# A decoder layer with a mixture of experts: cross attention with unpacked token rows joined in, and the order of the first expert loads

## The chip, the cores and the metric

The kernel runs on one core of one Trainium2 chip. The metric is the device time in microseconds (us) of one execution. Engines are named as in the profile: PE is TensorE, ACT is ScalarE, DVE is VectorE, POOL is GpSimd, SP is SyncE, which here only issues DMAs.

## The reference, cut to what matters

Two sequences of 1024 tokens with 256 features go through self-attention, cross attention (16 heads, 64 keys) and a mixture of 16 experts, each followed by a residual sum and a layer norm. What the change touches is the router and what follows it:

```
x = layernorm(x + xattn(x, ctx, mask))               # x2 of the kernel
logits = x @ router_w + router_b                      # 16 experts
probs  = softmax(logits)
topw, topi = top_k(probs, 4)
topw = topw / sum(topw)
out[token] = sum over its 4 experts e of topw_e * (gelu(x @ w1[e] + b1[e]) @ w2[e] + b2[e])
x = layernorm(x + out)
```

## The kernel before

The 2048 tokens are 16 tiles of 128 (NT = 16). The kernel has these stages: setup and projections, self-attention, cross attention with the router, a table of expert steps, the expert loop, and a last norm. Every engine has its own program; they meet through counting semaphores.

**Cross attention** is a software pipeline. On each engine the function `pipeline(engine, 16, [(skew, fn), ...])` runs steps t = 0, 1, ...; in step t it calls `fn(t - skew)` in the listed order, if that tile exists. The list is thus the order of the work on that engine, and the largest skew says how many steps follow the last tile. The first steps are written out, the middle ones run in a hardware loop in which tile numbers are registers, and the last ones are written out again. An optional `ramp` list holds for the first `RAMP` steps.

For tile t, on PE: `cquery` (skew 0), `cscores` (1, line 799 begins it), `cturn_p` (2), `cattend` (2, line 821), `turn_o` and `project` (3), then with x2 known `turn_x2` (4), `logits` (4), and `positions` (6), which counts with two small matmuls how many earlier tokens chose each expert. On DVE: `head_max`, `sub_max` (1), `head_inv`, `head_norm` (2), the second norm (3, `residual2` to `norm2`, whose inverse root is `root2` on POOL), and the router (4 to 6): logits, their maximum, the probabilities, the four largest, a one-hot mask, the shares, the rows, and `indices`. ACT copies PSUM results to SBUF and takes exponentials (`cexps`, `rexps`).

**Dispatch.** Each token row has to be written to four places of the DRAM buffer `expert_rows`, one for each of its experts. ACT's `pack` copies the tile four times into the buffer `xd` (two tiles deep), where DVE puts beside each copy the token's own number (column D) and its share for that expert (column D + 1). POOL's `dispatch` (skew 6) issues four indirect DMAs for each tile, 16 x 4 in all (line 563). `pack` of tile t and `indices` of tile t wait until the four scatters of tile t - 2 have landed, because they reuse its buffers.

**Between the stages.** DVE makes a table `tab` (18 small steps) of which rows and which expert each expert step takes. PE sums each token's shares times b2 (`turn_shares`, `bias_sums`, in two halves), ACT copies the sums to `total`, SP stores the first half (2 x 512 KB, after `xb` 4) and ACT the second (2 x 512 KB). SP then loads w1 and w2 of the first expert, waits for all scatters, and loads the rows of the first two expert steps (`load_rows`).

**Expert loop**, up to 48 steps, 40 here, each with 256 rows of one expert (w1, w2, rows loaded two steps ahead by SP): `turn_g`, `up`, gelu, `down`. ACT's `y_out` scales each result row by its share, `home_on[:, p, c, 1:2]`, and POOL adds the rows to `expert_sum` by an indirect DMA (line 582). POOL's first of these waits until all stores of the sums have landed. `y_out` also waits for the scatters of two steps before.

```
def done(t):      return t + 1 + BIAS       # semaphore value when tile t is done
def freed(t):     return t + 1              # when tile t - 2 is done
def upto(t, n):   ...                       # t + n, at most the last tile
```

## Time and profile before

| | us |
|---|---|
| median of 3 runs (lowest, highest) | 618.08 (615.75, 623.73) |
| the profiled execution, its own time | 615.27 |
| its span in the profile | 613.5 |
| PE busy in the span | 526.4 (86%) |
| DVE, ACT, POOL busy | 422.0, 344.0, 286.2 |

The span is the time from the first to the last instruction of the profiled execution. The page also gives a chain of work that ended last (PE 68%, DMA 7%, DVE 7%, POOL 4%, ACT 3%), and its strip of 40 slices shows PE's busy share at nine tenths nearly throughout, with a dip in slices 20 and 21, about 291 to 322 us, in which PE's clock is at its lower level too. A matmul's end is modelled, so PE can look busy where it is not at its peak.

### The profile page before, as it was taken

The page shows a single profiled execution, that of the slowest core. Times are in us where ns is not written, and L with a number is a line of the kernel's source. Part 1 is how long each engine was busy: PE and PEld are TensorE (multiplying, and loading weights), DVE is VectorE, ACT ScalarE, POOL GpSimd, SP SyncE. Part 2 cuts the span into 40 slices and gives each one's busy share as a digit, 9 for nine tenths or more (in the row PEclk, how much of TensorE's full clock was granted, in tenths as well). Part 3 has the DMA queues.
Part 4 walks back from the last instruction along what each step waited for, and adds up shares of the span by engine and source line. Part 5 has one row for each costly group of instructions (what it writes and reads, how often), then busy time and mean ns, then how long its engine had stood idle before and what let it go on. Part 6 is the DMA issues. An engine that isn't in the chain of part 4 may idle for free.

```text
span 613.5 us, 14428 instructions
## 1 busy us (share of the span) xinstructions
PE 526.4 (86%) x4048; PEld 497.8 (81%) x4048; DVE 422.0 (69%) x1053; ACT 344.0 (56%) x633; POOL 286.2 (47%) x264
## 2 busy tenths in 40 slices
PE   5999999999779999996327999999999999999700
PEld 4988888888669988886226999999999999999600
DVE  2646655555467888886534988888888787888336
ACT  2433333333235666664234777788778877778504
POOL 6551111111120356666640355666676767676733
PEclk9999999999989999999556999999999999999955
DMA  8799999400000132322387799999999999998477
GB/s 274 269 399 398 396 396 398 154 0 0 1 1 2 37 109 73 114 96 105 118 279 244 204 251 264 259 253 260 257 258 258 258 258 254 256 257 220 48 200 236
DMA packets 91836, 124.42 MB, mean 203 GB/s; under 512 B 6737, under 2 KB 62993, under 8 KB 91809
## 3 DMA queue, kind: packets, MB, share of 16 engines
q1 hardware_dynamic: 75264, 103.40, 51.4%
q0 software_dynamic: 14592, 19.41, 15.8%
q10 hardware_dynamic: 1952, 1.28, 0.8%
q8 instruction: 13, 0.21, 0.1%
q14 instruction: 15, 0.11, 0.1%
HBM read 61.93 MB, written 62.14 MB: 202 GB/s over the span
## 4 chain that ended last, share of the span: by engine, by line
PE 68%; issue 8%; DMA 7%; DVE 7%; POOL 4%; ACT 3%; POOLq 0%; SPq 0%; DVEq 0%; ACTq 0%
PE ps L347 18%; PE ps L349 18%; PE ps L348 18%; DMA expert_rows<-xd,idx 4%; POOL expert_rows L563 3%; PE ps L931 3%; PE ps L748 2%; PE ps L821 1%; DMA expert_sum<-yb,home_row 1%; PE ps L811 1%; PE ps L782 1%; DMA x_all<-in_x 1%; PE ps L852 1%; DMA total<-expert_sum 1%; PE ps L803 1%
## 5 line engine op out<-in xcount | busy, mean ns | idle before, releaser
L582 POOL DMA_INDIRECT expert_sum<-yb,home_row x80 | 163.1, 2039 | 107.4 <-DVE home_row L1513 62.3
L347 PE MATMUL ps<-gT_h,w_h 128*128 128x256 f32 x320 | 94.8, 296 | 1.8 <-issue 1.3
L347 PE MATMUL ps<-w_h,h_h 128*128 128x256 f32 x320 | 90.8, 284 | 1.9 <-DVE h_l L1506 1.9
L348 PE MATMUL ps<-gT_l,w_h 128*128 128x256 f32 x320 | 91.6, 286 | 0.0
L349 PE MATMUL ps<-gT_h,w_l 128*128 128x256 f32 x320 | 91.5, 286 | 0.0
L349 PE MATMUL ps<-w_h,h_l 128*128 128x256 f32 x320 | 90.6, 283 | 0.0
L348 PE MATMUL ps<-w_l,h_h 128*128 128x256 f32 x320 | 90.6, 283 | 0.0
L563 POOL DMA_INDIRECT expert_rows<-xd,idx x64 | 62.6, 978 | 33.4 <-issue 22.3
L1506 DVE TENSOR_TENSOR h_l<-hf,h_h 128x1024 fp32r<-128x1024 f32 x40 | 49.0, 1226 | 38.0 <-ACT h_h L1138 37.7
L1131 ACT ACTIVATE hf<-ps,b1s 128x256 f32<-128x256 f32 x160 | 62.8, 480 | 19.7 <-PE ps L349 19.3
L347 PEld LDWEIGHTS ps<-gT_h,w_h 128*128 128x128 f32 x320 | 62.2, 194 | 2.4 <-issue 1.5
L347 PEld LDWEIGHTS ps<-w_h,h_h 128*128 128x128 f32 x320 | 61.4, 192 | 2.4 <-DVE h_l L1506 2.4
L348 PEld LDWEIGHTS ps<-gT_l,w_h 128*128 128x128 f32 x320 | 62.3, 195 | 0.0
L349 PEld LDWEIGHTS ps<-gT_h,w_l 128*128 128x128 f32 x320 | 62.2, 194 | 0.0
L349 PEld LDWEIGHTS ps<-w_h,h_l 128*128 128x128 f32 x320 | 61.5, 192 | 0.0
L348 PEld LDWEIGHTS ps<-w_l,h_h 128*128 128x128 f32 x320 | 61.5, 192 | 0.0
L536 POOL TENSOR_TENSOR rstd<-ve,mhalf 128x1 f32<-128x1 f32 x16 | 8.8, 550 | 104.4 <-DVE ve L1209 104.4
L1113 ACT ACTIVATE yb<-ps,home_on 128x256 f32<-128x256 f32 x80 | 33.5, 470 | 37.9 <-DMA expert_sum<-yb,home_row 30.9
L1480 DVE TENSOR_TENSOR w_l<-w1f,w_h 128x1024 fp32r<-128x1024 f32 x40 | 49.0, 1225 | 1.4
L1485 DVE TENSOR_TENSOR w_l<-w2f,w_h 128x1024 fp32r<-128x1024 f32 x40 | 48.7, 1216 | 0.7 <-ACT w_h L1124 0.7
L347 PE MATMUL ps<-v_h,pT_h 128*128 (+1 forms) x128 | 37.1, 290 | 7.3 <-ACT x1T L1026 5.6
L1138 ACT ACTIVATE h_h<-hf 128x1024 fp32r<-128x1024 f32 x40 | 42.4, 1060 | 1.3
(241 smaller groups left out, 1342.7 us busy)
## 6 DMA issues: line engine op xcount, KB each, us to landing
expert_rows<-zeros SPq DMA_DIRECT2D x32, 1088.0 KB, 13.8
w1f<-in_L_ffn_w SPq DMA_DIRECT2D x40, 512.0 KB, 4.8
w2f<-in_L_ffn_w SPq DMA_DIRECT2D x40, 512.0 KB, 6.1
xg<-expert_rows SPq DMA_DIRECT2D x40, 272.0 KB, 3.9
total<-expert_sum SPq DMA_DIRECT2D x16, 256.0 KB, 5.8
x_all<-in_x SPq DMA_DIRECT2D x8, 256.0 KB, 6.9
expert_sum<-x_all SPq DMA_DIRECT2D x8, 256.0 KB
out<-ot SPq DMA_DIRECT2D x8, 256.0 KB, 2.6
```

The source lines that it names most:

```text
L347: pe.matmul(o, ah, bh, start=first, stop=False)
L348: pe.matmul(o, ah, bl, start=False, stop=False)
L349: return pe.matmul(o, al, bh, start=False, stop=last)
L563: pool.indirect_dma_start(out=xg_dram, out_offset=bass.IndirectOffsetOnAxis(ap=idx[:, p, r:r + 1], axis=0), in_=xd[:, p, r], in_offset=Non ...
L582: pool.indirect_dma_start(out=sums[p], out_offset=bass.IndirectOffsetOnAxis(ap=home_row[:, p, c:c + 1], axis=0), in_=yb[:, p, c], in_offse ...
L931: mm = pe.transpose(ps[:, p, kc * SLOT + c * P:kc * SLOT + (c + 1) * P], xg[:, p, c, kc * P:(kc + 1) * P], ident[:])
L1113: ins = act.activation(yb[:, p, c], ps[:, 6 + p, c * D:(c + 1) * D], ACT.Copy, scale=home_on[:, p, c, 1:2])
L1131: ins = act.activation(hf[:, p, j], ps[:, 2 + 2 * p + j // 2, (j % 2) * SLOT:(j % 2 + 1) * SLOT], ACT.Gelu, bias=b1s[:, j, ds(t, 1)])
L1138: act.activation(h_h[:, p], hf[:, p], ACT.Copy).then_inc(hh, 1)
L1480: dve.tensor_tensor(w1_l[:, p], w1f[:, p], f(w1_h[:, p]), ALU.subtract).then_inc(w1l, 1)
L1485: dve.tensor_tensor(w2_l[:, p], w2f[:, p], f(w2_h[:, p]), ALU.subtract).then_inc(w2l, 1)
L1506: dve.tensor_tensor(h_l[:, p], hf[:, p], f(h_h[:, p]), ALU.subtract).then_inc(hl, 1)
```

## The change

One row of `x_all`, 288 values wide, now holds a tile's token with all that its scatters need: 256 features, its 16 shares (columns D to D + E - 1, zero where an expert wasn't chosen) and its number (column HOME = D + E). `xd` and `pack` are gone: all four scatters of a tile send the same row of `x_all`, and `idx` has a place for every tile, so nothing waits for earlier scatters. `y_out` picks its share from 16 columns with the expert's number, which ACT loads into a register. The router works on logits: the largest four are found on them, ACT negates the first (`neg_max`), and a second exponential (`top_sum`) sums the four. `positions` moves from skew 6 to 4 (another PSUM bank), `dispatch` and `indices` from 6 to 5, `head_inv` and `head_norm` from 2 to 3 at the head of DVE's step, `turn_x2` from 4 to 3 at the end of PE's step. POOL's steps are all written out, and in the last ones half a tile's scatters go before `root2`. `bias_sums` of the first half comes after the last tile's `positions` instead of the third last's. ACT's order changes, with `q_out` ahead of `cexps` in a ramp of 4 steps. SP loads w2 of the first expert after the first two sets of rows, and stores the second half of the b2 sums itself, after w1 of the second step.

```diff
-RW = D + 16
+RW = D + 2 * E
+HOME = D + E
...
-RAMP = 3
+RAMP = 4
...
-        x_all = sb("x_all", [P, NT, D])
+        x_all = sb("x_all", [P, NT, RW])
+        idx = sb("idx", [P, NT, K], U32)
...
-        home_i = sbe("home_i", [P, 2, K], I32)
+        home_i = sbe("home_i", [P, NT], I32)
...
-        idx = sbe("idx", [P, 2, K], U32)
-        xd = sbe("xd", [P, 2, K, RW])
...
@@ SyncE @@
             first = expert_of(0)
             load_up(0, 0, first)
-            load_down(0, 0, first)
...
             for t in range(2):
                 load_rows(t, t, places[t])
+            load_down(0, 0, first)
...
                     load_up(t, p, expert_of(t))
+                if isinstance(t, int) and t == 1:
+                    sp.wait_ge(xb, 8)
+                    for b in range(B):
+                        store_tiles(sp, sums[1], total, b * TPB + 4, 4)
...
@@ GpSimd @@
-            pool.memset(xd[:], 0.0).then_inc(c_pool, 1)
+            pool.memset(x_all[:, :, D:RW], 0.0).then_inc(c_pool, 1)
...
-            pool.tensor_copy(xd[:, :, :, D], home_i[:]).then_inc(c_pool, 1)
+            pool.tensor_copy(x_all[:, :, HOME], home_i[:]).then_inc(c_pool, 1)
...
+            def send(t, p, k, r):
+                pool.indirect_dma_start(
+                    out=xg_dram, out_offset=bass.IndirectOffsetOnAxis(ap=idx[:, t, r:r + 1], axis=0),
+                    in_=x_all[:, p * TPB + k], in_offset=None).then_inc(sc_dma[p][r], 16)
+
+            def ready(t):
+                pool.wait_ge(lidx, done(t))
+                pool.wait_ge(lsh, done(t))
+                pool.wait_ge(x2k, done(t))
+                pool.sem_inc(passed, 1)
...
+            def dispatch_first(t, p, k):
+                ready(t)
+                for r in range(K // 2):
+                    send(t, p, k, r)
+
+            def dispatch_rest(t, p, k):
+                for r in range(K // 2, K):
+                    send(t, p, k, r)
+
+            steady = [(1, causal), (3, root2), (5, dispatch)]
+            ending = [(5, dispatch_first), (3, root2), (5, dispatch_rest)]
...
-            pipeline(pool, NT, [(1, causal), (3, root2), (6, dispatch)])
+            for t in range(NT + 5):
+                for skew, fn in steady if t < NT + 1 else ending:
+                    if 0 <= t - skew < NT:
+                        fn(t - skew, (t - skew) % 2, (t - skew) // 2)
...
@@ TensorE @@
             def turn_o(t, p, k):
                 pe.wait_ge(co, done(t))
                 pe.wait_ge(coc, freed(t) + 1)
+                if not (isinstance(t, int) and t < 2):
+                    pe.wait_ge(lcar, done(t - 2))
...
             def project(t, p, k):
...
-                if not (isinstance(t, int) and t < 4):
-                    pe.wait_ge(lcar, done(t - 4))
+                pe.wait_ge(x2t, freed(t) + 1)
...
-                    mm = pe.transpose(ps[:, 4, D + kc * P:D + (kc + 1) * P], xs[:, p, kc * P:(kc + 1) * P], ident[:])
+                    mm = pe.transpose(ps[:, 7, D + kc * P:D + (kc + 1) * P], xs[:, p, kc * P:(kc + 1) * P], ident[:])
...
-                if isinstance(t, int) and t == NT - 3:
+                pe.wait_ge(coc, done(upto(t, 1)))
+                pe.matmul(ps[:, 6, D:D + E], tri_r[:], mk[:, p], start=True, stop=True)
+                pe.matmul(ps[:, 6, D + E:D + 2 * E], ones_r[:], mk[:, p], start=True, stop=True).then_inc(pos_ps, 1)
+                if isinstance(t, int) and t == NT - 1:
                     pe.wait_ge(cpc, done(NT - 1))
                     bias_sums(0, 0)
...
-            pipeline(pe, NT, [(1, cscores), (3, turn_o), (4, turn_x2), (2, cturn_p), (6, positions), (3, project),
-                              (0, cquery), (4, logits), (2, cattend)])
+            pipeline(pe, NT, [(1, cscores), (4, logits), (3, turn_o), (2, cturn_p), (3, project), (0, cquery),
+                              (2, cattend), (4, positions), (3, turn_x2)])
...
@@ ScalarE @@
-            def pack(t, p, k):
-                act.wait_ge(x2k, done(t))
-                if not (isinstance(t, int) and t < 2):
-                    for r in range(K):
-                        act.wait_ge(sc_dma[p][r], 16 * k)
-                act.sem_inc(passed, 1)
-                act.activation(xd[:, p, :, 0:D], x_all[:, ds(p * TPB + k, 1), :].broadcast_to([P, K, D]), ACT.Copy).then_inc(xdc, 1)
...
+            def neg_max(t, p, k):
+                act.wait_ge(l8, done(t))
+                act.activation(lmax[:, p:p + 1], mx8[:, p, 0:1], ACT.Copy, scale=-1.0).then_inc(lmx, 1)
...
-                act.activation(lexp[:, p], lg[:, p], ACT.Exp, bias=lmax[:, p:p + 1], accum_out=lsum[:, p:p + 1]).then_inc(lex, 1)
+                act.activation(lexp[:, p], lg[:, p], ACT.Exp, bias=lmax[:, p:p + 1]).then_inc(lex, 1)
...
+            def top_sum(t, p, k):
+                act.wait_ge(lwi, freed(t))
+                act.activation(top[:, p], mx8[:, p, 0:K], ACT.Exp, bias=lmax[:, p:p + 1], accum_out=wsum[:, p:p + 1]).then_inc(lws, 1)
...
-            pipeline(act, NT, [(3, o_out), (4, x2_turned), (2, p_out), (1, cexps), (0, q_out), (5, pack), (4, keep_x2), (4, rexps)],
-                     ramp=[(3, o_out), (4, x2_turned), (2, p_out), (0, q_out), (1, cexps), (5, pack), (4, keep_x2), (4, rexps)], ramp_steps=RAMP)
+            pipeline(act, NT, [(4, x2_turned), (4, keep_x2), (3, o_out), (2, p_out), (4, neg_max), (4, rexps), (1, cexps), (4, top_sum), (0, q_out)],
+                     ramp=[(4, x2_turned), (4, keep_x2), (3, o_out), (2, p_out), (0, q_out), (4, neg_max), (4, rexps), (1, cexps), (4, top_sum)], ramp_steps=RAMP)
...
-            act.wait_ge(xb, 8)
-            for b in range(B):
-                store_tiles(act, sums[1], total, b * TPB + 4, 4)
...
             def y_out(t, p, k):
...
+                expert = act.value_load(tab[1:2, ds(t, 1)], min_val=0, max_val=E - 1)
...
-                    ins = act.activation(yb[:, p, c], ps[:, 6 + p, c * D:(c + 1) * D], ACT.Copy, scale=home_on[:, p, c, 1:2])
+                    ins = act.activation(yb[:, p, c], ps[:, 6 + p, c * D:(c + 1) * D], ACT.Copy, scale=home_on[:, p, c, ds(expert, 1)])
...
@@ VectorE @@
-            def logits_max(t, p, k):
-            def router_inv(t, p, k):
-            def router_probs(t, p, k):
...
-                dve.max(mx8[:, p], rp[:, p]).then_inc(l8, 1)
+                dve.max(mx8[:, p], lg[:, p]).then_inc(l8, 1)
...
-                dve.tensor_reduce(wsum[:, p:p + 1], mx8[:, p, 0:K], AX.X, ALU.add).then_inc(lws, 1)
...
+            def share_sum(t, p, k):
+                dve.wait_ge(lws, done(t))
+                dve.reciprocal(winv[:, p:p + 1], wsum[:, p:p + 1]).then_inc(lwi, 1)
+
             def all_shares(t, p, k):
-                dve.wait_ge(lmk, done(t))
-                dve.scalar_tensor_tensor(shares[:, ds(p * TPB + k, 1), 0:E].rearrange("p a e -> p (a e)"), rp[:, p], winv[:, p:p + 1],
+                dve.wait_ge(lwi, done(t))
+                dve.wait_ge(lex, done(t))
+                dve.scalar_tensor_tensor(shares[:, ds(p * TPB + k, 1), 0:E].rearrange("p a e -> p (a e)"), lexp[:, p], winv[:, p:p + 1],
+                                         f(mk[:, p]), ALU.mult, ALU.mult).then_inc(lst, 1)
+                dve.scalar_tensor_tensor(x_all[:, ds(p * TPB + k, 1), D:D + E].rearrange("p a e -> p (a e)"), lexp[:, p], winv[:, p:p + 1],
                                          f(mk[:, p]), ALU.mult, ALU.mult).then_inc(lsh, 1)
...
-                for r in range(K):
-                    if not (isinstance(t, int) and t < 2):
-                        dve.wait_ge(sc_dma[p][r], 16 * k)
-                dve.tensor_copy(idx[:, p], slotf[:, p]).then_inc(lidx, 1)
-                dve.tensor_scalar(xd[:, p, :, D], xd[:, p, :, D], float(P), None, ALU.add).then_inc(dest, 1)
-                dve.wait_ge(lwi, done(t))
-                dve.tensor_scalar(xd[:, p, :, D + 1], mx8[:, p, 0:K], winv[:, p:p + 1], None, ALU.mult).then_inc(lw, 1)
+                dve.tensor_copy(idx[:, ds(t, 1), :].rearrange("p a r -> p (a r)"), slotf[:, p]).then_inc(lidx, 1)
...
-            pipeline(dve, NT, [(5, router_inv), (1, head_max), (5, router_probs), (1, sub_max), (5, largest), (3, residual2),
-                               (5, chosen), (3, stats2), (5, chosen_float), (6, rows_of), (3, aggr2), (6, next_rows), (5, one_hot),
-                               (3, var2), (6, pick_rows), (5, chosen_mask), (6, slots), (5, all_shares), (6, indices),
-                               (3, norm2), (2, head_inv), (2, head_norm), (4, logits_out), (4, logits_max)])
+            pipeline(dve, NT, [(3, head_inv), (5, rows_of), (3, head_norm), (5, next_rows), (5, pick_rows), (5, slots), (5, indices),
+                               (1, head_max), (4, logits_out), (4, largest), (1, sub_max), (3, residual2), (4, chosen), (3, stats2),
+                               (4, chosen_float), (3, aggr2), (4, one_hot), (3, var2), (4, chosen_mask), (4, share_sum), (4, all_shares),
+                               (3, norm2)])
...
-                dve.tensor_copy(home[:, p], xg[:, p, :, D:D + 2]).then_inc(hm, 1)
+                dve.tensor_copy(home[:, p], xg[:, p, :, D:HOME + 1]).then_inc(hm, 1)
```

## Rows read from the trace of the kernel before

**Rows 1.** Busy time by stretch: us, PE, PEld, DVE, ACT, POOL busy, clock, DMA share, GB/s

```profile
310.00:320.00 10.00, 2.22 (x10) 1.87 (x10) 1.10 (x6) 2.08 (x5) 4.36 (x5) 0.50 1.00 315
...
360.00:560.00 200.00, 200.00 (x1682) 200.00 (x1682) 167.06 (x259) 157.08 (x291) 134.72 (x64) 1.00 0.99 257
```

**Rows 2.** Timeline of PE in cross attention: start, length, instruction, idle before

```profile
181.22 0.50 PE L799 MATMUL ps<-hide_r,ones_r 64*128 64x512 f32 x2
...
182.51 0.44 PE L828 MATMUL ps<-ident,octx 128*128 128x128 f32 x2
...
205.54 1.95 PE L821 MATMUL ps<-vb,cpT 128*128 128x34 f32 x16
...
219.32 1.95 PE L821 MATMUL ps<-vb,cpT 128*128 128x34 f32 x16
...
269.78 1.95 PE L821 MATMUL ps<-vb,cpT 128*128 128x34 f32 x16
271.67 0.51 PE L799 MATMUL ps<-hide_r,ones_r 64*128 64x512 f32 x2
```

**Rows 3.** Waits from 205 to 280 us: who for whom, total, times, longest

```profile
ACT xd L1076 <- DMA expert_rows<-xd,idx: 16.4, 10, 2.0
```

**Rows 4.** Timeline of ACT, cross attention, before its loop

```profile
183.86 1.02 ACT L1049 ACTIVATE cpT<-ps 128x1024 f32<-128x1024 f32 x1 [0.49 <-PE ps L811]
...
195.02 0.31 ACT L1084 ACTIVATE lexp<-lg,lmax 128x16 f32<-128x16 f32 x1 [2.24 <-DVE lmax L1350]
195.24 0.19 ACT L1084 ACTIVATION_READ_ACCUMULATOR lexp<-lg,lmax 128x1 f32 x1
...
204.70 1.06 ACT L1059 ACTIVATE prob<-prob 128x1024 f32<-128x1024 f32 x1 [0.28 <-DVE prob L1304]
```

**Rows 5.** Timeline of DVE, before its loop

```profile
182.63 1.23 DVE L1299 TENSOR_REDUCE hmax<-ps 128x16 f32<-128x1024 f32 x1 [0.59 <-PE ps L803]
...
186.27 0.15 DVE L1335 TENSOR_SCALAR ve<-mv 128x1 f32<-128x1 f32 x1
...
206.54 0.23 DVE L1391 SCALAR_TENSOR_TENSOR shares<-rp,winv,mk 128x16 f32<-128x16 f32 x1
206.69 0.16 DVE L1418 CAST idx<-slotf 128x4 uint32<-128x4 f32 x1
```

**Rows 6.** Timeline of DVE, inside its loop

```profile
235.53 0.23 DVE L1391 SCALAR_TENSOR_TENSOR shares<-rp,winv,mk 128x16 f32 x1
235.83 0.17 DVE L1418 CAST idx<-slotf 128x4 uint32<-128x4 f32 x1
```

**Rows 7.** Timeline of POOL, the last tiles

```profile
286.31 1.04 POOL L563 DMA_INDIRECT expert_rows<-xd,idx  x1 [0.82 <-issue]
287.65 0.96 POOL L563 DMA_INDIRECT expert_rows<-xd,idx  x1 [0.30 <-issue]
...
292.29 0.57 POOL L553 TENSOR_TENSOR rstd<-ve,mhalf 128x1 f32<-128x1 f32 x1 [1.14 <-DVE ve L1335]
```

**Rows 8.** Chain of waits into the expert loop: start, length, what

```profile
290.18 2.46 DMA expert_rows<-xd,idx
...
314.62 7.18 DMA expert_rows<-xd,idx
322.16 2.94 DMA xg<-expert_rows
```

**Rows 9.** Issues of SP's queue: start, length, DMA

```profile
309.45 0.98 SPq L354 DMA_DIRECT2D expert_sum<-total  x2
313.24 0.40 SPq L415 DMA_DIRECT2D w1f<-in_L_ffn_w  x1
```

**Rows 10.** Timeline of DVE, the end of the step table

```profile
311.38 0.20 DVE L1467 CAST tab<-ps 2x48 int32<-2x48 f32 x1 [0.47 <-PE ps L915]
```

**Rows 11.** Issues of SP in the expert loop

```profile
363.37 0.38 SPq L410 DMA_DIRECT2D xg<-expert_rows  x1
364.65 0.37 SPq L415 DMA_DIRECT2D w1f<-in_L_ffn_w  x1
```

More of the change, by code:

```diff
@@ L279, in decoder_layer @@
         xg = sbl("xg", [P, 2, 2, RW])
-        home = sbl("home", [P, 2, 2, 2])
-        home_on = sbl("home_on", [P, 2, 2, 2])
+        home = sbl("home", [P, 2, 2, E + 1])
+        home_on = sbl("home_on", [P, 2, 2, E + 1])
         home_row = sbl("home_row", [P, 2, 2], U32)
@@ L817, in cattend @@
                 pe.wait_ge(co, freed(t) + 1)
-                if not (isinstance(t, int) and t < 3):
-                    pe.wait_ge(lgb, done(t - 3))
+                if not (isinstance(t, int) and t < 2):
+                    pe.wait_ge(lgb, done(t - 2))
                 for g, pair in enumerate(SCORED):
@@ L826, in turn_o @@
                 pe.wait_ge(coc, freed(t) + 1)
+                if not (isinstance(t, int) and t < 2):
+                    pe.wait_ge(lcar, done(t - 2))
                 for kc in range(KD):
@@ L848, in project @@
                 pe.wait_ge(cres, freed(t) + 1)
-                if not (isinstance(t, int) and t < 4):
-                    pe.wait_ge(lcar, done(t - 4))
+                pe.wait_ge(x2t, freed(t) + 1)
                 for kc in range(KD):
```

70 lines of the change are left out of this document (25 added, 45 removed).

## The prediction

> **What bounds the kernel now.** I read the busy time by stretch first. In the expert loop, 360 to 560 us, PE is busy all 200 us, ACT only 157.08 [rows 1]; the stretch holds 1682 matmuls at 52 a step (48 and 4 transposes), so 32.3 steps of 6.19 us, and PE sets them. Nothing of the change is PE work there. From 310 to 320 us PE works 2.22 of 10 us while the DMA engines are busy all the time [rows 1]: the expert loop can't start before the last scatters have landed and the first rows are loaded. That gap is what the change can shorten.
>
> The timeline of PE shows cross attention. Its steps, from one `cattend` (line 821) to the next, last 6.89 us before the loop of registers ((219.32 - 205.54) / 2) and 7.21 us in it ((269.78 - 219.32) / 7) [rows 2]. The waits name the reason: ACT's `pack` stood 16.4 us, in 10 waits, for scatters of two tiles before [rows 3].
>
> The last tiles on POOL show the real chain: a scatter takes 0.96 us with 0.30 to the next, the first after a `root2` comes 0.82 after it [rows 7]. A tile costs 1.34 + 2 x 1.26 + 0.96 = 4.8 us, and `pack` and `indices` wait for landings on top, until the last scatter starts at 314.62. It lands 7.18 us later, one at 290.18 took 2.46; then SP issues `xg` at 322.16, which lands after 2.94, and PE starts at 325.1 [rows 8].
>
> **Cross attention's steps.** Removed on ACT: `pack`, and its wait. Removed on DVE: six small instructions (maximum, inverse, probabilities, sum, two on `xd`); added: a second `all_shares`. ACT gains `neg_max` and `top_sum`. The new order makes a cycle that I add from the start of `cscores` (line 799). PE comes to `turn_o` 1.29 later [rows 2], now with `logits` between (0.35, my estimate for two transposes' worth of work): 1.64. From `turn_o` to ACT's `p_out` takes 183.86 - 182.51 = 1.35 [rows 2, 4]: 2.99. `p_out` 1.0, `neg_max` and `rexps` 0.22 each by the small exponential's step from 195.02 to 195.24 [rows 4]: 4.4. `cexps` 1.0, `top_sum` 0.22 and its accumulator read 0.19 [rows 4]: 5.8. This read is what `share_sum` waits for on DVE. Its reciprocal 0.2, two `all_shares` at 0.15 each [rows 5], the norm 0.4, `turn_x2` 0.2 on PE, and `cscores` follows: 6.95. PE's own work is the 6.89 of above. In the loop an instruction with a register in its address costs DVE 0.30 instead of 0.15 to the next [rows 5, 6]; two such and the norm behind them add 0.3, so 7.25. Seven or eight loop steps go from 7.21 to 7.25, and some written-out steps get 0.06 and one `positions` (0.2) more: **0.5 us lost** by the last step. Bounds: 6.89 everywhere would gain 7 x 0.32 = 2.2; 7.6, if the waits between engines add up, would lose about 4.
>
> POOL isn't the limit there: `root2` 0.57, gap 0.82, scatters 4.8, together 6.2 us [rows 7]. Its addresses are plain numbers, all steps being written out.
>
> **The last tiles.** Step 16 starts at 271.67 [rows 2]. `ve` comes 1.41 + 3.64 us after `cscores` began (182.63 - 181.22, 186.27 - 182.63) [rows 2, 5], with the router's parts between 0.1 more, so `root2` of tile 13 starts at 276.9. Tile 11's scatters: 278.3 to 283.1. Two of tile 12: 283.4 to 285.7. `root2` of tile 14 to 286.2; before, it ended 0.82 ahead of 286.31, at 285.5 [rows 7]. Two of tile 12 from 287.1, two of tile 13 from 289.6 to 291.9. `root2` of tile 15 started at 292.29 before [rows 7]; now its tile is held 0.7 by the former `root2` and 0.4 by `logits`, put ahead: 293.4. Rest of 13: 294.8 to 297.1. Tile 14: 297.4 to 302.2. Tile 15: 302.5, its last scatter starts at 306.4. The rows of 14 and 15 are ready by about 295 and 300, so POOL sets this. That is 8.2 us ahead of 314.62: one tile less was left, and two landings are no longer waited for.
>
> **The landing.** Before, two stores of 512 KB by SP were issued at 309.45, two by ACT after them, w1 at 313.24 and w2 behind it [rows 9]: 3 MB around the last scatter, which took 4.7 us more than the one at 290.18 [rows 8]. After, the first half of the sums follows the last tile's `positions`. I put it at 304.3, the table at 305.2, w1 at 306.9 (as 311.58 to 313.24 before [rows 9, 10]). So 1.5 MB lie around the scatter. Bounds are 2.46 and 7.18; the nearer row is the crowded one, since the stores precede the scatters by as little. I take 5.2, so 311.6. The rows' load comes 0.36 later and takes 2.94 [rows 8]: PE starts at 314.9, **10.2 us earlier**. Against this stands a rule. The Trainium skill, "DMA: Bandwidth & Descriptors", section "Queues, rings and completion order", says that each DMA engine goes round between the queue rows that have work, a packet at a time. By it what slows a scatter is that another queue is active, not how many bytes it holds; the rival below prices this from rows.
>
> w1 lands in time: issued at 306.9, even with 7.18 it is there at 314.1 and DVE's split is over before `up`, which needs the turned rows, some 2.5 us behind 314.9. PE's granted clock was 0.50, the 1.2 GHz level, from 310 to 320 [rows 1], after a stretch with little PE work; I leave it so in the first `up`.
>
> **w2 and the late stores.** SP now issues w2 at about 312.9, w1 of step two, then 1 MB of sums. 1.5 MB move to where the loop's first loads are. At the 315 GB/s of rows 1 they take 4.8 us. w2 is needed only by the first gelu's stage, 8 us after the rows, and the sums only by POOL's first accumulation, over 20 us later. The third rows, behind the stores, may be late: 0 to 2 us, I take **0.5 lost**. If that cover is gone, `gelus`, queued behind `w2_high` on ACT, waits, and `down` with it.
>
> **The expert loop.** `y_out` gets a `value_load` on ACT. The trace of ACT has none; SP's load of rows to load of w1 holds one, 364.65 - 363.37 - 0.38 = 0.90 us with two waits [rows 11]. I take 0.9 as the dearest likely, below it 0. ACT has (200 - 157.08) / 32.3 = 1.33 idle a step [rows 1], part of it a wait for a landing that comes behind the load, so the 40 steps lose nothing; the last result pays it: **0.9 lost**. The Trainium skill, the same page, section "Latency and other measured facts", gives a floor of about 0.6 us for a tensor load; by it the last step would pay 0.6, an estimate from that page. Rows of 288 instead of 272 values add 16 KB a step, 1% of what the DMA engines move in 6.19 us at 257 GB/s [rows 1], with loads two steps ahead: nothing; with no such cover 0.06 a step, 2.5. `home` with 34 instead of 4 columns stays under 0.1 on DVE, which is idle 33 of 200 us. The zeros' 6% more ends long before cross attention. Setup saves POOL one long memset, which nobody waits for.
>
> **Sum.** 10.2 - 0.5 - 0.5 - 0.9 = 8.3 us. Against the profiled execution's 615.27 (span 613.5) this is 607.0. The median of the runs stands 2.8 above that execution; from 618.08 it is 609.8. I say **608**, chance 0.38, own range 605.5 to 611.
>
> **Rivals.**
> - All covers hold: the step is 6.89 (+2.7 against my loss of 0.5), the landing 2.7 (+2.5), no crowding (+0.5), the load hidden (+0.4). 14.4 us, **602**. For it speaks that the wait of rows 3 goes. 0.22.
> - The landing stays at 7.18, since any active queue slows the scatter (the rule above): 2 us less, **610**. 0.18.
> - The cross step is set by the way over `top_sum`: at 7.6 us, 11 steps lose 0.4 each instead of 0.5 in all: **612**. Against it: ACT has over 2 us free in such a step once `pack` is gone. 0.10.
> - The reordering doesn't do what it says: w2 and the sums only move the crowd behind the rows, the first gelu waits for w2. A landing of 7.18 from 312.9, then `w2_high` and the gelu's table, ends just at `up`'s end; 3 us more cost 3: **611**. 0.07.
> - Slower: the `value_load` on ACT holds the loop. It decides from 1.33 us on; at 1.54 the 8.3 are gone (8.3 / 40 = 0.21), at 1.85 the kernel is over 2% slower, at 2.0 it takes 27 - 8 = 19 more, **636**. Against it: the 0.90 of rows 11. 0.05.
>
> **The numbers.** Range: 601 takes in most of the first rival, 614 the second to fourth; outside are the slow rival and the ends. 2% of 618.08 is 12.4 us, about what a measurement can tell from no change, so faster means below 605.7: nearly all of the first rival and the forecast's edge, 0.27. Slower 0.04. Same 0.69.
>
> **What would show it.** `cattend` to `cattend` in the loop (7.25); last scatter's start (306.4) and landing (5.2); PE's first transpose of rows (314.9); the expert step (6.19); ACT's gap before the last `yb`. I am wrong if POOL waits between the last tiles' scatters, if the step is off by over 0.2, or if the expert step grows.

## The result, and the profile after

| | before | after |
|---|---|---|
| median of 20 runs each, same chip (us) | 616.74 | 613.66 |
| lowest, highest | 614.85, 623.73 | 608.77, 623.99 |
| the profiled execution (span) | 615.27 (613.5) | 613.05 (611.2) |
| PE, DVE, ACT, POOL busy | 526.4, 422.0, 344.0, 286.2 | 535.9, 419.1, 336.2, 289.8 |

The ratio is 0.9935, 95% interval 0.9911 to 0.9959: 4.0 us faster, between 2.5 and 5.5 (3.1 by the medians), where 8.3 were forecast. The time of the new kernel lies in the range of 601 to 614, at its upper end, 5.7 us above the 608 that I said. Times of one kernel fall into groups some 3 us apart, each with its own mean granted clock (after: 612.03 to 614.57 at 0.931 to 0.937, 616.67 to 617.31 at 0.926 to 0.928), so below a span is read with its clock and steps are compared one by one, and each ratio is of the executions within 1.5% of their kernel's fastest.

The page of after: busy time of each engine, then slices of 15.3 us with PE's busy tenths and its granted clock.

```profile
PE 535.9 (88%) x4048; PEld 501.5 (82%) x4048; DVE 419.1 (69%) x973; ACT 336.2 (55%) x650; POOL 289.8 (47%) x264
...
PE   5999999999779999999648999999999999999600
...
PEclk9999999999989999978657999999999999999955
```

PE is busy 9.5 us longer with the same 4048 matmuls. No matmul was added; some ran at the lower clock. The slice with a 7 in the clock's strip, 260 to 275 us, is in the middle of cross attention, where the page of before has a 9.

**Cross attention.** PE's timeline, `cattend` (now line 839), the counterpart of [rows 2]:

```profile
235.68 1.87 PE L839 MATMUL ps<-vb,cpT 128*128 128x34 f32 x16
...
242.93 1.87 PE L839 MATMUL ps<-vb,cpT 128*128 128x34 f32 x16
...
257.63 1.87 PE L839 MATMUL ps<-vb,cpT 128*128 128x34 f32 x16
...
268.36 1.87 PE L839 MATMUL ps<-vb,cpT 128*128 128x34 f32 x16
...
275.42 1.87 PE L839 MATMUL ps<-vb,cpT 128*128 128x34 f32 x16
...
278.01 0.50 PE L817 MATMUL ps<-hide_r,ones_r 64*128 64x512 f32 x2
```

Steps of 7.25 and (257.63 - 242.93) / 2 = 7.35, then one of 10.73, then 7.06; the last row is `cscores` of step 16 (line 817), 271.67 before. The windows of that stretch (us, PE, PEld, DVE, ACT, POOL busy, clock, DMA share, GB/s) say what the long one is:

```profile
258.00:260.00 2.00, 1.84 (x17) 1.75 (x17) 1.74 (x12) 1.02 (x4) 1.11 (x2) 1.00 0.01 2
...
262.00:264.00 2.00, 2.00 (x10) 1.35 (x9) 1.22 (x2) 0.00 (x0) 1.63 (x2) 0.50 0.38 148
...
266.00:268.00 2.00, 2.00 (x9) 1.64 (x9) 0.21 (x1) 1.97 (x4) 0.00 (x0) 0.62 0.00 0
```

The clock is 1.00 (2.4 GHz) to 260 us, 0.50 (1.2 GHz) about 261 to 267, and 1.00 again. One step's matmuls take twice as long, and the step is 10.73 - 7.45 = 3.28 us longer than its neighbour. PE had been busy 1.84 of the 2 us before the fall.

The chain of waits gives the terms of an ordinary step in the loop (start, length, what):

```profile
231.03 0.50 PE ps L817 x2
...
232.95 0.26 PE ps L848 x2
...
234.12 0.04 ACT cpT L1067
...
235.49 0.04 ACT prob L1077
...
236.44 0.38 ACT top L1105 x2
...
236.84 0.17 DVE winv L1394
...
237.46 0.42 DVE xs L1358
...
237.92 0.44 PE ps L882 x2
```

It is the cycle of the forecast: scores, logits, `turn_o`, ACT's `p_out`, two small ACT instructions, `cexps`, `top_sum`, DVE's reciprocal, shares and norm, and PE's transposes of x2. PE's own order closes it: `turn_x2` ends its step, and the next `cscores` stands behind it.

In the written-out steps, 7.12 to 7.15 us long, the chain is put down to PE alone, but there too `turn_x2` starts only when DVE's norm is done, at 194.20:

```profile
193.79 0.41 DVE L1358 TENSOR_SCALAR xs<-yres,mv,rstd 128x256 f32<-128x256 f32 x1
```

```profile
194.26 0.44 PE L882 MATMUL ps<-ident,xs 128*128 128x128 f32 x2
```

The chain's piece for the logits, and PE's weight loads for them (idle before in brackets):

```profile
195.99 0.55 PE ps L890 x4
196.54 0.27 PE ps L848 x2
```

```profile
195.92 0.52 PEld L890 LDWEIGHTS ps<-rw,x2T 128*128 128x128 f32 x4 [0.33 <-issue]
```

The weights of the logits are loaded only after a gap of 0.33, which PE then sees: 0.55, where the same piece takes 0.35 in experiment 7.

**The last tiles.** POOL's timeline: the first scatter of tile 11, `root2` of tile 15, the last scatter. It answers to [rows 7].

```profile
284.48 1.14 POOL L558 DMA_INDIRECT expert_rows<-x_all,idx  x1 [0.27 <-DVE x_all L1401]
...
299.72 0.57 POOL L555 TENSOR_TENSOR rstd<-ve,mhalf 128x1 f32<-128x1 f32 x1 [1.56 <-DVE ve L1352]
...
312.06 0.96 POOL L558 DMA_INDIRECT expert_rows<-x_all,idx  x1 [0.30 <-issue]
```

From tile 11's first scatter to the last are 27.6 us (312.06 - 284.48), against 28.1 forecast (306.4 - 278.3). All of it merely starts late. The clock falls once more here, to 0.57 from 284 to 292 us, where before kept 1.00 until 288; PE's last step lies in it, 8.50 us long (6.94 before).

**Into the loop.** The chain of waits, the counterpart of [rows 8], then SP's issues, that of [rows 9], and PE's transposes of expert rows:

```profile
312.06 4.81 DMA expert_rows<-x_all,idx
...
323.15 6.43 DMA xg<-expert_rows
```

```profile
310.39 0.94 SPq L352 DMA_DIRECT2D expert_sum<-total  x2
...
317.23 1.00 SPq L408 DMA_DIRECT2D xg<-expert_rows  x2
...
320.65 1.01 SPq L352 DMA_DIRECT2D expert_sum<-total  x2
323.15 0.69 SPq L408 DMA_DIRECT2D xg<-expert_rows  x1
```

```profile
320.11 2.21 PE L949 MATMUL ps<-ident,xg 128*128 128x128 f32 x8 [6.67 <-DMA xg<-expert_rows]
...
329.63 1.12 PE L949 MATMUL ps<-ident,xg 128*128 128x128 f32 x4 [2.58 <-DMA xg<-expert_rows]
...
337.10 0.60 PE L949 MATMUL ps<-ident,xg 128*128 128x128 f32 x4
...
343.29 0.60 PE L949 MATMUL ps<-ident,xg 128*128 128x128 f32 x4
```

The last scatter lands in 4.81 us, not 7.18. PE has rows at 320.11, 5.0 us earlier than before. The third rows are issued behind the sums at 323.15 and take 6.43 us: PE waits 2.58. The expert step is 6.19 (343.29 - 337.10), as before. The steady loop starts from 337.10, which in the trace of before reads

```profile
340.10 0.60 PE L931 MATMUL ps<-ident,xg 128*128 128x128 f32 x4
```

so 3.0 us are left there, and 2.3 at the end. ACT's last results but one, after and before (idle ahead in brackets):

```profile
574.53 0.84 ACT L1130 ACTIVATE yb<-ps,home_on 128x256 f32<-128x256 f32 x2 [0.93 <-PE ps L347]
```

```profile
576.70 0.84 ACT L1113 ACTIVATE yb<-ps,home_on 128x256 f32<-128x256 f32 x2 [0.22 <-PE ps L349]
```

The `value_load` shows as the 0.93 against 0.22: 0.7 us.

### The profile page after: what moved, and what is told of

The parts are those of the page before. It is cut to its first block, busy times and chain, and to the rows that moved or that the text cites. A ratio compares the mean times of both kernels' runs of the same rounds, so it can differ in the third digit from the quotient of the medians.

```text
span 611.2 us, 14540 instructions
## 1 busy us (share of the span) xinstructions
PE 535.9 (88%) x4048; PEld 501.5 (82%) x4048; DVE 419.1 (69%) x973; ACT 336.2 (55%) x650; POOL 289.8 (47%) x264
## 4 chain that ended last, share of the span: by engine, by line
PE 75%; issue 7%; DVE 5%; DMA 4%; POOL 4%; ACT 3%; SPq 1%; ACTq 0%; POOLq 0%; DVEq 0%
PE ps L345 19%; PE ps L347 18%; PE ps L346 18%; PE ps L949 3%; POOL expert_rows L558 3%; PE ps L821 2%; PE ps L829 2%; PE ps L768 2%; PE ps L839 1%; PE ps L890 1%; PE ps L817 1%; DMA xg<-expert_rows 1%; PE ps L800 1%; PE ps L882 1%; DMA x_all<-in_x 1%
## 5 line engine op out<-in xcount | busy, mean ns | idle before, releaser
L602 POOL DMA_INDIRECT expert_sum<-yb,home_row x80 | 167.4, 2093 | 103.5 <-DVE home_row L1514 81.7
L558 POOL DMA_INDIRECT expert_rows<-x_all,idx x64 | 63.3, 989 | 19.0 <-issue 17.2
L1141 ACT ACTIVATE w_h<-w2f 128x1024 fp32r<-128x1024 f32 x40 | 42.7, 1067 | 1.7 <-DMA w2f<-in_L_ffn_w 1.7
```

The lines of the kernel that those rows point to most:

```text
L558: pool.indirect_dma_start(out=xg_dram, out_offset=bass.IndirectOffsetOnAxis(ap=idx[:, t, r:r + 1], axis=0), in_=x_all[:, p * TPB + k], in_ ...
L602: pool.indirect_dma_start(out=sums[p], out_offset=bass.IndirectOffsetOnAxis(ap=home_row[:, p, c:c + 1], axis=0), in_=yb[:, p, c], in_offse ...
L1141: act.activation(w2_h[:, p], w2f[:, p], ACT.Copy).then_inc(w2h, 1)
```

## The experiments

Each is compared with the kernel before on the same chip. Where a short name helps, "the change" is the changed kernel.

**1. The norm ahead of the shares.** One edit of the change's list on DVE:

```diff
-  (4, chosen_mask), (4, share_sum), (4, all_shares), (3, norm2)])
+  (4, chosen_mask), (3, norm2), (4, share_sum), (4, all_shares)])
```

> The changed kernel with one move on DVE: norm2 comes before share_sum and all_shares. Theory A (the cycle through top_sum and the two shares sets the step): the norm no longer waits for ACT's accumulator read; what is left is root2 (ve at 236.42, root2 to 237.23, norm2 at 237.26 at the earliest where it began at 237.46), so the step goes from 7.35 to 7.15 us in the loop, the last scatter starts 2 us earlier, and the time falls by about 2 us, or by about 5 if the low-clock step at 260 to 269 us goes too. Rival B (POOL's root2, not the shares, holds the norm): the step stays at 7.3 and the time within 0.5 us of the changed kernel.

Measured: 615.56 us median of 12, ratio 0.9934 (0.989 to 0.9978), the change's own. In the profile (of the execution of 618.34) steps written out went from 7.13 to 7.04, in the loop from 7.45 and 7.25 to 7.30 to 7.43 and 7.06 to 7.24. The terms behind `top_sum` were worth 0.1 to 0.2 us only: with them out of its way, the norm starts little earlier, since it now waits for POOL's `root2` (0.45 to 0.47 us, idle DVE). That is the rival's reason, though not its 7.3. The cycle over PE has to be cut elsewhere.

**2. PE's waits filled.** Three transposes of the identity into a free place, ahead of `turn_x2`'s wait for x2:

```diff
+  pe.wait_ge(cqc, done(upto(t, 3)))
+  for i in range(3):
+      pe.transpose(ps[:, 4, D:D + P], ident[:], ident[:])
```

> The changed kernel with three extra 128-column transposes on PE, into unused PSUM, ahead of turn_x2's wait: 0.33 us of work where PE otherwise waits for the norm, for each of 16 tiles. Theory C (PE's waits in the longer step are what lets its granted clock fall to 1.2 GHz for one step, 3.3 us, in most executions): the low-clock step in cross attention goes in the profile, most runs lie near the single fastest run of the changed kernel (608.8), and the time falls by 2 to 3 us though PE does 5 us more work. Rival D (the drop has another cause): it stays, and the time is the same or up to 2 us longer.

Measured: 612.07 median of 7, ratio 0.9884 (0.9813 to 0.9954); four at 609.45 to 612.07 with clock 0.941 to 0.948, three at 618.82 to 620.52 with 0.924 to 0.926. In the profile, which is of the 618.82, the loop's steps are 7.26 and 7.45 to the last, none long. A step of 10.19 is the very first, at the entry to cross attention; the very last is long too (8.25, its `cattend` 3.47 for 1.87). A window at the place where the change's clock falls:

```profile
262.00:266.00 4.00, 3.89 (x35) 3.60 (x36) 3.54 (x21) 2.53 (x8) 1.96 (x3) 1.00 0.14 48
```

Work for nothing keeps the clock up in the middle, though the step isn't shorter.

**3. w2 and the late sums where they were**, in the change: w2 ahead of the scatters' wait, the second half of the sums by ACT.

```diff
             load_up(0, 0, first)
+            load_down(0, 0, first)
...
-            load_down(0, 0, first)
...
-                if isinstance(t, int) and t == 1:
-                    sp.wait_ge(xb, 8)
-                    for b in range(B):
-                        store_tiles(sp, sums[1], total, b * TPB + 4, 4)
@@ ScalarE @@
+            act.wait_ge(xb, 8)
+            for b in range(B):
+                store_tiles(act, sums[1], total, b * TPB + 4, 4)
```

> The changed kernel with w2 of the first expert loaded ahead of the rows and the second half of the b2 sums stored by ACT, both as in the kernel before. Theory E (moving 1.5 MB behind the rows pays: the landing of the last scatter went from 7.2 to 4.8 us): the landing is 7 us again, the third rows arrive without the 2.6 us wait of PE, and the kernel is 1 to 2 us slower than the changed one. Rival F (it only moves the crowd): the landing is longer, the third rows come in time, and the time is within 0.5 us of the changed kernel.

Measured: 619.43 median of 12, ratio 1.0015 (0.9972 to 1.0058): by the ratio nothing of the gain is left. Its chain has

```profile
327.63 5.83 DMA xg<-expert_rows
```

and PE gets its rows 11.6 us after the last scatter's start (333.51 - 321.89), where the change takes 8.05. But the landing is not 7 us again, as theory E had it. The last scatter lands in 5.1 us here; it is the first rows that take 5.83 to load instead of 2.9. ACT's two stores, here and then in the kernel before, where the last scatter started at 314.62:

```profile
322.53 1.87 ACTq L352 DMA_DIRECT2D expert_sum<-total  x2
```

```profile
311.78 1.72 ACTq L354 DMA_DIRECT2D expert_sum<-total  x2
```

Here they are issued behind the last scatter, there 2.8 us ahead of it. The crowd is the same, but what it holds up is what comes behind it.

The profile (625.1 at clock 0.919) had three long steps, so its span is no measure, and the ratio holds such steps too: only two of the 12 executions had a clock of 0.930 or more, against 13 of the change's 20. Those two took 614.82 and 615.09, where the change took 613.69 to 614.57 at 0.931 to 0.933. At like clocks the old places cost about 1 us, an estimate from these few.

**4. The late sums later**: at the fourth step of the expert loop.

```diff
-                if isinstance(t, int) and t == 1:
+                if isinstance(t, int) and t == 3:
```

> The changed kernel with the two late stores of the b2 sums (1 MB) issued by SP two expert steps later, after w1 of the fourth step. Theory G (the third rows are late because they queue behind these stores: 6.4 us to land, PE waits 2.6 us): xg of the third step lands in 4 us, PE's wait before its transposes goes, and the time falls by 1.5 to 2.5 us. Rival H (w1 and w2 crowd them anyway): PE still waits over 1.5 us there, and the time falls by less than 1 us. POOL's first accumulation waits for the stores at about 341 us; issued by 331 they are in time.

Measured: 616.22 median of 12, ratio 0.9976 (0.9939 to 1.0013), which overlaps the change's. The profiled execution, though, had the change's pattern of clocks and steps, and so can be laid beside it: last scatter at 312.08, and

```profile
328.10 0.89 PE L949 MATMUL ps<-ident,xg 128*128 128x128 f32 x4
...
335.29 0.60 PE L949 MATMUL ps<-ident,xg 128*128 128x128 f32 x4
```

No wait for the third rows, and the steady loop 1.8 us earlier than 337.10. So much the sums' place costs, in the trace; the median can't show it: ten of these 12 executions ran at a mean clock of 0.929 or below. The two others took 611.10 and 611.11 at 0.935 and 0.936, where the change has 612.03 and 612.15 at 0.935.

**5. Only the move of w2 and the sums**, in the kernel before (the edits of experiment 3, the other way about).

> The kernel before with one part of the change alone: w2 of the first expert behind the first two sets of rows, and the second half of the b2 sums stored by SP behind w1 of the second step. Theory E (this part shortens the last scatter's landing, then is partly given back at the third rows): landing from 7.2 to about 4.8 us, PE's first transpose of rows about 2 us after the landing less than before, third rows late by up to 2.5 us, in all 0 to 1.5 us faster. Rival F (it only moves the crowd): the time is within 0.5 us of the kernel before.

Measured: 616.22 median of 12, ratio 0.9992 (0.9956 to 1.0028), lowest 612.15 and 612.30. Span 610.4 at 0.943 in the profile, 3.1 below before's. Cross attention is unchanged, with the last scatter at 314.65 for 314.62:

```profile
314.65 3.81 DMA expert_rows<-xd,idx
...
324.72 5.85 DMA xg<-expert_rows
```

The landing falls from 7.18 to 3.81 and the third rows are late as in the change. This move alone brings in the trace as much as the whole change does, and the steady loop starts 3.2 us earlier (336.86 for 340.10); by the medians of both kernels neither half can be told from nothing alone.

**6. The `value_load` twice.**

```diff
                 expert = act.value_load(tab[1:2, ds(t, 1)], min_val=0, max_val=E - 1)
+                expert = act.value_load(tab[1:2, ds(t, 1)], min_val=0, max_val=E - 1)
```

> The changed kernel with the register load on ACT in y_out done twice in every expert step. Theory I (ACT has about 1.3 us free in a step, and the load costs it 0.9 only where it waits for PE last, in the drain): the expert step stays at 6.19 us, the last yb starts 0.8 us later after PE, and the time grows by 0.5 to 1.5 us in all. Rival J (the load already used up ACT's slack): the step grows by 0.4 us or more, 15 us in all.

Measured: 617.05 median of 10, ratio 0.9978 (0.9939 to 1.0018); two long steps in the profile. The expert step did not move:

```profile
340.80 0.60 PE L949 MATMUL ps<-ident,xg 128*128 128x128 f32 x4
...
346.99 0.60 PE L949 MATMUL ps<-ident,xg 128*128 128x128 f32 x4
```

ACT had room for a second load in every step, as [rows 1] had said; that excludes the slow rival. The gap before ACT's last results but one grew from 0.93 to 1.78, so there a load costs some 0.8.

**7. A new order of cross attention**, with experiment 4's later sums. PE does `turn_x2` right behind `cscores`, where the norm of the step before is long done, and the logits behind `cturn_p`; ACT takes `cexps`, DVE `sub_max`, ahead of the router's parts.

```diff
@@ TensorE @@
-  [(1, cscores), (4, logits), (3, turn_o), (2, cturn_p), (3, project), (0, cquery),
-   (2, cattend), (4, positions), (3, turn_x2)]
+  [(1, cscores), (4, turn_x2), (3, turn_o), (2, cturn_p), (4, logits), (3, project), (0, cquery),
+   (2, cattend), (4, positions)]
@@ ScalarE @@ (the ramp likewise, with q_out ahead of cexps)
-  [(4, x2_turned), (4, keep_x2), (3, o_out), (2, p_out), (4, neg_max), (4, rexps), (1, cexps), (4, top_sum), (0, q_out)]
+  [(4, keep_x2), (4, x2_turned), (3, o_out), (2, p_out), (1, cexps), (4, neg_max), (4, rexps), (4, top_sum), (0, q_out)]
@@ VectorE @@
-  (1, head_max), (4, logits_out), (4, largest), (1, sub_max), (3, residual2)
+  (1, head_max), (1, sub_max), (4, logits_out), (4, largest), (3, residual2)
```

> The changed kernel with the cycle cut: turn_x2 of a tile moves from the end of PE's step to behind the next step's cscores, logits behind cturn_p, on DVE sub_max ahead of the logits, on ACT cexps ahead of the three small router steps; the two late stores two expert steps later, as in e4. Theory A (norm2, root2 and top_sum, ahead of cscores on PE, made the step): the step falls from 7.13 and 7.35 us to about 6.9, PE's own work, the last scatter starts 3 to 4 us earlier than in the changed kernel, and the time falls by 4 to 5 us against e4, more if the low-clock step goes. Rival K (the next wait, head_norm and next_rows ahead of turn_o, takes its place): the step stays above 7.2 and the time within 1.5 us of e4.

Measured: **601.96 median of 5 (601.43 to 604.5), ratio 0.9773 (0.9733 to 0.9814)**, faster than both kernels. The steps are 6.86 to 6.88 from the third to the last but two, PE's own work, and none is long:

```profile
233.41 1.87 PE L839 MATMUL ps<-vb,cpT 128*128 128x34 f32 x16
...
240.27 1.87 PE L839 MATMUL ps<-vb,cpT 128*128 128x34 f32 x16
```

```profile
262.00:266.00 4.00, 4.00 (x36) 3.55 (x36) 3.62 (x14) 1.36 (x5) 3.12 (x4) 1.00 0.39 136
```

The last scatter starts at 302.74, 9.3 us earlier than in the change and in experiment 4 (312.08). 3.3 of it is the low-clock step that is gone; the other 6.0 are more than the 3 to 4 that I expected.

**8. The fillers with the later sums** (edits 2 and 4 together).

> e4 (late stores two steps later) with the three extra transposes of e2 ahead of turn_x2's wait: the same kernel as e4 but for PE's work in its waits. Theory C (those waits let the granted clock fall in the middle of cross attention): no step of 10.7 us after the fourth in the profile, and the mean clock of most runs 0.940 or more where most runs of e4 have 0.921 to 0.929; the time falls by 3 us against e4 in the middle of the runs. Rival D: the clocks are spread as those of e4, and the time is the same or up to 2 us longer.

Measured: 612.24 median of 12, ratio 0.991 (0.987 to 0.995), in two groups of six: 607.69 to 610.09 at clock 0.945 to 0.946, and 614.39 to 617.45 at 0.927 to 0.929. The profile, of the second group, has one long step of 10.4, the first of cross attention, none in the middle, and a last one of 8.26 at clock 0.50. So the lower clock has more than one place, the entry, the middle and the end; fillers in the steps cover the middle alone. Half of the executions reach a clock of 0.940, not most.

**9. The new order without the later sums**: experiment 7 with the stores back in step two.

> The kernel with the new order of cross attention, but with the late b2 stores back at the second step of the expert loop, where the change has them. It tells the order's gain from the stores'. If the two are independent: cross attention's steps stay at 6.87 us, the last scatter starts at 302.7, and only the third set of rows is late again, with about 2.6 us of waiting on PE and 1.9 us on the whole, so 604 us (ratio 0.980). Rival: most of what the new order gave came with the later stores; then the time goes back by 4 us or more, towards 606 or above.

Measured: 606.56 median of 6, ratio 0.9836 (0.9783 to 0.9888); three runs at 603.03 to 603.14 (clock 0.938 to 0.947) and three at 609.98 to 610.16 (0.932). The profile's steps are 6.87 and its span 601.3, 1.7 above experiment 7's. The wait for the third rows is back, which accounts for the difference:

```profile
320.89 0.66 PE L949 MATMUL ps<-ident,xg 128*128 128x128 f32 x4 [2.65 <-DMA xg<-expert_rows]
```

In the profile the order and the stores add up, as forecast, with the last scatter at 303.16; so they do in the faster three, 1.6 us above the 601.43 to 602.14 of experiment 7. The median alone would speak for the rival (606 or above), by three executions at a lower clock; where it fell in them no trace shows.

**10. Of the new order, ACT's and DVE's part alone**: experiment 7, but `turn_x2` at the end of PE's step.

```diff
-  [(1, cscores), (4, turn_x2), (3, turn_o), ... (2, cattend), (4, positions)]
+  [(1, cscores), (3, turn_o), ... (2, cattend), (4, positions), (3, turn_x2)]
```

> The kernel with the new order, but the transposes of x2 back at the end of PE's step and the logits at its head, as the change has them; ACT's and DVE's new orders stay. Theory: a step is a cycle over PE, ACT and DVE that is closed by these transposes at the end of PE's step, so steps go back to 7.1 us written out and 7.3 in the loop, the last scatter starts 3 us or more later than 302.7, PE's waits at the end of each step bring back a step of 10 us at the low clock in some executions, and the time is 606 to 612. Rival: the orders of ACT and DVE were what mattered (exponentials ahead of the router's small ones); then steps stay at 6.9 and the time at 602.

Only `turn_x2` differs from experiment 7: other than the expectation says, the edit leaves the logits behind `cturn_p`.

Measured: 610.54 median of 9, ratio 0.99 (0.9864 to 0.9936). Steps 7.16 written out, 7.3 and 7.5 in the loop, one of 9.12 (and 10.01 at the entry); last scatter at 313.51:

```profile
232.25 1.87 PE L839 MATMUL ps<-vb,cpT 128*128 128x34 f32 x16
...
241.37 1.87 PE L839 MATMUL ps<-vb,cpT 128*128 128x34 f32 x16
```

In its written-out steps the chain runs round DVE, from `head_max` over the shares to the norm, `turn_x2` and `cscores`: another cycle, closed by the same two transposes.

**11. PE's part alone**: the change with experiment 4's stores and PE's list of experiment 7.

> The change's kernel with its late b2 stores later, and of the new order only PE's: the transposes of x2 behind cscores, the logits behind cturn_p; ACT and DVE keep the orders of the change. It stands against the last but one, which has ACT's and DVE's alone. Theory: moving the transposes takes them off the end of PE's step, but with ACT's x2_turned at the head of its step and the DVE's sub_max behind the router's largest, part of a cycle stays: steps 6.9 to 7.1 us and 602 to 607. Rival: ACT waits for the transposes ahead of o_out and p_out, and PE waits for p_out; then steps go over 7.2 and the time is 610 or more.

Measured: 606.58 median of 6, ratio 0.9835 (0.9794 to 0.9875). Steps 6.87, every second in the loop 7.06 to 7.12:

```profile
233.12 1.87 PE L839 MATMUL ps<-vb,cpT 128*128 128x34 f32 x16
...
239.99 1.87 PE L839 MATMUL ps<-vb,cpT 128*128 128x34 f32 x16
```

The last step was long here (8.91, its `cattend` taking 3.47 us, the clock 0.50 from 278 to 290), as in the change (8.50); it is 5.9 in the four experiments in which ACT and DVE have the new order (7, 9, 10, 12). It can be 7.2 with the old one too (experiments 1 and 3), where the clock fell later. Experiments 10 and 11 settle the ordinary steps: one edit of PE's list takes them from 7.3 or 7.4 to 6.9 or 7.0, and the edits of ACT and DVE are worth 0.1 us a step on top.

**12. No half tiles at the end**: experiment 7 with POOL's steady order throughout.

```diff
-                for skew, fn in steady if t < NT + 1 else ending:
+                for skew, fn in steady:
```

> The kernel with the new order, but POOL keeps its steady order to the end: root2 before all four scatters of a tile, no half tiles. The prediction took the half tiles as told and priced nothing for them. Theory: POOL's work is the same 4.8 us a tile and it is the bound in the last four tiles, so the last scatter starts within 1 us of 302.7 and the time is the same. Rival: root2 of the last tiles comes later behind four scatters than behind two, DVE's norm and PE's logits follow it, and the last scatter starts 2 us or more later.

Measured: 605.49 median of 5 (599.72 to 605.8), ratio 0.9796 (0.9755 to 0.9837), not to be told from experiment 7. The profile's last scatter starts at 301.44, 1.3 us earlier:

```profile
286.55 0.57 POOL L555 TENSOR_TENSOR rstd<-ve,mhalf 128x1 f32<-128x1 f32 x1
```

Here the last `root2` finds its input ready. With half tiles it starts at 290.39 after a wait of 0.91 with scatters queued behind it. Half tiles gain nothing that shows; I was right to price them at nothing. Of the 1.3 us against them 0.8 stood before the last tiles (last `cattend` at 279.01 for 279.78), and 0.5 is one profile's word. Experiments 7, 9, 11 and 12 all beat both kernels. Twelve's 599.72 is the lowest time of all, seven's median the best.

## Why the prediction was right or wrong

The forecast against the two profiled executions, in us later (+) or earlier (-), each line the difference between two points of the traces:

| part | forecast | measured |
|---|---|---|
| cross attention, to `cscores` of step 16 (271.67 before, 278.01 after) | +0.5 | +6.3 |
| from there to the last scatter (42.95, 34.05) | -8.2 | -8.9 |
| from there to PE's first rows (10.53, 8.05) | -2.0 | -2.5 |
| from there to the steady loop (14.95, 16.99) | +0.5 | +2.0 |
| the rest | +0.9 | +0.7 |
| sum | -8.3 | -2.3 |

**Wrong: "Cross attention's steps ... 0.5 us lost."** This term is 5.8 of the 6.0 us missed; the other lines cancel. It lost 6.3, in two parts. The first is the length of the ordinary steps. The four written-out ones behind the first took 7.13 each, where they had 6.57 to 6.88: 1.5 us. I had given them PE's 6.89 and 0.06, the 6.95 of the cycle. But the cycle came to 7.13 and held PE there already: `turn_o` starts 1.76 behind `cscores` for my 1.64, the logits' weights being late between them, and `cscores` 0.36 behind `turn_x2` for my 0.2, the transposes' own work. In the loop the cycle came to 7.25, as I said, but in every second step only. In the others `cscores` starts 0.57 behind `turn_x2` and not 0.37, so 7.45; 1.3 us in eight steps. The other terms held in the loop: `turn_o` 1.77 behind `cscores` for 1.64, `p_out` 1.32 behind that for 1.35, then 0.93 and 0.95 for 1.0 each, 0.40 for 0.41. Another 0.7 comes at step 16, whose `cscores` now stands behind `turn_x2`, and 0.4 is won ahead of the first step.

The second part, 3.3 us, I had no step for: the long step at 1.2 GHz. By my own sign of being wrong (a step off by over 0.2), this is the step: 10.73 for 7.25. I read the clock of the gap between the stages and never asked whether the new waits could bring it down inside one. In the profiles all five kernels with the change's PE order and unfilled waits (the change, experiments 1, 3, 4, 6) have one or two such steps mid-stage, and so has experiment 10, with 9.12. The five in which the waits are filled or `turn_x2` is moved (2, 7, 8, 9, 12) have none there; the last step is at the low clock in 2, 8 and 11, and in part in the change. Experiments 2 and 8, which fill these waits and touch nothing else, show that the waits at that place bring it on, by the clocks of all executions more than by their two profiles: 10 of their 19 have a mean clock of 0.940 or more, against 1 of the 66 of the five unfilled kernels. Why they do stays open: before waits more (PE busy 9.52 of the 10 us from 250 on, the change 9.68) and keeps its clock.

**The cause of the cycle is shown, not only argued.** Experiment 11 moves `turn_x2` and the logits on PE alone, and the steps fall to 6.87, PE's work, and 7.1 in every second one of the loop; experiment 10 has `turn_x2` where the change has it and all the rest moved, and they don't. The third rival (the way over `top_sum`, 7.6) named the right cycle; it was 7.35 in the loop, and a shorter way behind `top_sum` brought 0.1 to 0.2 (experiment 1).

**Right: the last tiles.** One tile less is left, and no scatter waits for earlier landings. 8.9 us came for 8.2; with its start 6.3 late, the last scatter came at 312.06 and not 306.4. The order of POOL's work was as written, the wait for the last root too (from 291.9 to 293.4 in the forecast, 1.56 in the trace).

**Right in size: the landing.** 4.81 for my 5.2, and experiment 5 shows that moving w2 and the late sums shortens it (7.18 to 3.81). The rival said 7.18 stays, after the rule of the Trainium skill, "DMA: Bandwidth & Descriptors", section "Queues, rings and completion order", that an engine goes round between active queue rows. As a price it was wrong: SP's queue was as active as ever. But the move also took ACT's two stores from ahead of the scatter, and with them a second queue: with stores in SP's queue alone the last scatters of all these traces land in 3.8 to 5.3, and only with ACT's ahead of them too in 7.2 and 7.6 (the last two of before). So these runs don't tell the bytes from the number of queues as the cause, and the rule isn't refuted. What they do show is that the order of issue counts: in experiment 3, with all 3 MB and both queues, but ACT's stores and the loads issued behind it, the last scatter landed in 5.1. I had counted what lies around it, ahead or behind.

**Mis-sized: "third rows ... 0.5 lost".** The mechanism was the one named; it cost 2.0 to the steady loop (1.8 by experiment 4), the upper end of the 0 to 2 that I had. The third load took 6.43 us behind 1 MB of sums, with w2 and w1 of the next step in the same stretch. w2 came late too: ACT's `w2_high` waited 0.73 us in the first step and 0.98 in the second, so the fourth rival was there as a symptom and too small to decide.

**Right: `value_load`.** It costs 0.7 at the end and nothing in the loop, where ACT's slack takes even two (experiment 6). The floor of about 0.6 for a tensor load that the Trainium skill has, "DMA: Bandwidth & Descriptors", section "Latency and other measured facts", is nearer than my 0.9. Rows of 288 values cost nothing that shows: 6.19 us a step in both.

**The first rival**, all covers hold at 602, is where experiment 7 ends (601.96), but not by its terms: the steps are its 6.89 and the third rows its 0, while the landing is 4.90 and not 2.7, and an earlier last scatter makes up for it. That the two numbers agree is luck.

## What to carry to other kernels

In a software pipeline, follow one item's chain back to the engine that it left, and see what stands behind its last instruction there: an instruction that waits for another engine at the end of a step puts its wait ahead of the next step's first work, and moving it behind the first work of the next step brought the last scatter 7.6 us forward here (312.08 in experiment 4, 304.52 in 11), 3.3 of it by the low-clock step that went with the waits. Price it by starts, from one instruction's start to the next one's, since what each is busy leaves out the weights that load late. Where PE is near its bound, ask of every new wait also what the clock does, and give the range the price of one step at half speed.

## What the runs showed that I had not expected

- PE's granted clock can fall to 0.50 for some 6 us in a stretch where PE is busy 92 to 97%: 3.3 us for one step of 7.4. Three dummy transposes a step kept it up in the middle of the stage.
- At the entry to cross attention the same fall stood in the profiles of experiments 1, 2, 3, 8 and 10 (first steps of 10.0 to 10.5 instead of 6.0), with and without fillers. The two groups of times in experiments 2 and 8, some 9 and 7 us apart, may come from it; one trace of the upper group in each shows the fall, and none that the lower group is without it.
- A 128-row scatter of 1088-byte rows landed in 2.46 us when little else moved, in 3.81 with two 512 KB stores issued 5.1 us ahead of it, and in 7.18 with 2 MB of stores and 1 MB of loads issued in the 5.2 us ahead of it; with 1152-byte rows and the stores 1.5 to 4.2 us ahead it was 4.72 to 5.30. A load of rows behind two 512 KB stores took 5.59 to 8.50 us instead of 2.8 to 3.1.
